# Layer 1 of a two-layer gated attention kernel: the two nearest prototypes taken from the products, their distances on ScalarE, residual rows in and results out two tiles at a time

## The reference, cut to what matters

```
def _L1_ffn_ref(x, prototypes, B, A, bias, temp):
    x2 = jnp.sum(xf * xf, axis=1, keepdims=True)
    p2 = jnp.sum(prototypes * prototypes, axis=1)
    d2 = x2 + p2[None, :] - 2.0 * (xf @ prototypes.T)
    dists = jnp.sqrt(jnp.maximum(d2, 0.0))
    t = jnp.maximum(jnp.abs(temp), 0.1)
    w = jax.nn.softmax(-dists / t, axis=1)
    topw, topi = jax.lax.top_k(w, 2)
    topw = topw / jnp.sum(topw, axis=1, keepdims=True)
    for tslot in range(2):
        idx = topi[:, tslot]
        h = jnp.einsum('nri,ni->nr', B[idx], xf)
        y = jnp.einsum('nor,nr->no', A[idx], h) + bias[idx]
        out = out + topw[:, tslot:tslot + 1] * y
...
x = x + jnp.tanh(g_xattn[1]) * _L1_xattn_ref(_layernorm(x, axis=-1), ctx_1024, ctx_1024, ...)
x = x + jnp.tanh(g_ffn[1]) * _L1_ffn_ref(_layernorm(x, axis=-1), ...)
```

## Time and profile before

| | us |
|---|---|
| median of 3 runs | 3044.14 |
| lowest and highest | 3039.18, 3046.79 |
| the profiled execution | 3044.48 |
| its span | 3042.8 |

### The profile page before, as it was taken

How to read it: one execution, slowest core, us unless ns; L and a number is a source line. 1 busy time by engine, 2 the same in 40 slices (tenths; PEclk the granted TensorE clock), 3 DMA queues, 4 the chain that set the end, 5 groups by cost and what they waited for, 6 DMA issues and landing times.

```text
span 3042.8 us, 96434 instructions
## 1 busy us (share of the span) xinstructions
PE 2739.6 (90%) x31534; PEld 2166.8 (71%) x31534; DVE 2507.4 (82%) x6126; ACT 1983.7 (65%) x4683; POOL 2089.8 (69%) x2777
## 2 busy tenths in 40 slices
PE   4888896899999999689699999999989999999996
PEld 2444444677777777557578888888878888888885
DVE  6877776688888888675689999899989989999885
ACT  2666666687777877575466666666656666666663
POOL 3893000567666676544388888888888888888886
PEclk9999998899999999899899999999999999999998
DMA  5987566223233232631567766666776767766663
GB/s 152 364 337 294 235 254 256 76 81 93 77 90 84 80 93 76 220 117 41 121 142 158 158 147 149 140 145 150 145 137 149 141 144 149 147 150 145 145 132 78
DMA packets 638943, 455.55 MB, mean 150 GB/s; under 512 B 389760, under 2 KB 612592, under 8 KB 633648
## 3 DMA queue, kind: packets, MB, share of 16 engines
q1 hardware_dynamic: 618288, 402.31, 52.2%
q0 software_dynamic: 7328, 23.40, 2.5%
q10 hardware_dynamic: 12960, 25.23, 2.2%
HBM read 235.08 MB, written 148.83 MB: 126 GB/s over the span
## 4 chain that ended last, share of the span: by engine, by line
PE 32%; DVE 6%; issue 4%; POOL 3%; SPq 2%; ACT 2%; DMA 1%; DVEq 0%; POOLq 0%; ACTq 0%
PE banks L150 10%; PE banks L152 9%; PE banks L151 9%; PE banks L1416 2%; DVE a_near L1540 2%; PE banks L1401 2%; SPq L1058 1%; DVE a_probT_lo L1492 1%; ACT a_qT_hi L1234 1%; DVE a_pick L1627 1%; DVE a_rsum L1504 1%; DVE a_wtop L1567 1%; POOL a_pn L1154 1%; DMA a_xnT<-a_xn_parts 0%; DMA a_hwT<-a_hw_parts 0%
## 5 line engine op out<-in xcount | busy, mean ns | idle before, releaser
L1234 ACT ACTIVATE a_qT_hi<-banks 128x512 f16<-128x512 f32 x252 | 150.4, 597 | 540.8 <-PE banks L152 540.8
L383 POOL TENSOR_TENSOR a_probT_lo<-a_expT,a_probT_hi 128x512 f16<-128x512 f32 x256 | 291.4, 1159 | 218.5 <-ACT a_probT_hi L466 218.5
L459 ACT ACTIVATE a_expT<-banks,a_top,w_score_scale 128x512 f32<-128x512 f32 (+1 forms) x384 | 272.4, 709 | 152.5 <-PE banks L550 146.1
L1154 POOL TENSOR_TENSOR a_pn<-a_prob,a_rsum 128x1024 f32<-128x1024 f32 (+1 forms) x256 | 310.2, 1233 | 5.8 <-DVE a_rsum L1506 5.8
L150 PE MATMUL banks<-a_xnT,w_q_hi 128*128 128x256 f16 x1024 | 281.2, 275 | 15.0 <-DMA a_xnT<-a_xn_parts 13.2
L150 PE MATMUL banks<-a_vo_front,a_probT_hi 128*128 128x256 f16 x1024 | 279.8, 273 | 9.4 <-DVE a_probT_lo L1492 6.5
L152 PE MATMUL banks<-a_xnT,w_q_lo 128*128 128x256 f16 x1024 | 280.6, 274 | 0.0
L151 PE MATMUL banks<-a_xnT,w_q_hi 128*128 128x256 f16 x1024 | 280.6, 274 | 0.0
L152 PE MATMUL banks<-a_vo_front,a_probT_lo 128*128 128x256 f16 x1024 | 279.7, 273 | 0.0
L151 PE MATMUL banks<-a_vo_front,a_probT_hi 128*128 128x256 f16 x1024 | 279.6, 273 | 0.0
L1490 DVE TENSOR_TENSOR a_qT_lo<-banks,a_qT_hi 128x512 f16<-128x512 f32 x252 | 172.0, 683 | 77.9 <-ACT a_qT_hi L1234 77.7
(11 more groups left out here) (380 smaller groups left out, 10177.7 us busy)
## 6 DMA issues: line engine op xcount, KB each, us to landing
vo<-kv_vo_out SPq DMA_DIRECT2D x38, 2048.0 KB, 8.1
a_vo_front<-vo SPq DMA_DIRECT2D x128, 512.0 KB
kt<-kv_k_out ACTq DMA_DIRECT2D x9, 2560.0 KB, 14.9
a_k<-kt SPq DMA_DIRECT2D x64, 308.0 KB, 3.5
kv_raw_e<-in_L_ffn_w POOLq DMA_DIRECT2D x16, 1024.0 KB, 8.9
a_x<-in_x SPq DMA_DIRECT2D x64, 256.0 KB, 2.9
a_y<-in_x SPq DMA_DIRECT2D x64, 256.0 KB, 2.7
x<-a_y SPq DMA_DIRECT2D x64, 256.0 KB, 2.8
```

What stands on the lines that cost most here:

```text
L383: pool.tensor_tensor(probT[b][1][:, first:end, :], expT[b][:, first:end, :], probT[b][0][:, first:end, :], ALU.subtract).then_inc(prob_rea ...
L459: act.activation(expT[1 - h][0:rows, first:end, :], bank, ACT.Exp, bias=top[0:rows, 0:1], scale=weights["score_scale"][0:rows, 0:1]).then_ ...
L1154: last = pool.tensor_tensor(keys_of(pn[h]), e[:, :, first:end], rsum[h][:, :].unsqueeze(2).broadcast_to([P, H, end - first]), ALU.mult)
L1234: act.activation(out, bank[:, 0:cols].rearrange("p (c s) -> p c s", c=out.shape[1]), ACT.Copy, scale=scale)\
```

## The change

`near` is gone. `nearest_two` looks for the largest of `dots` itself, and the row's squared length comes in later, on ScalarE, for the two found values alone: `square_gaps` computes relu(ysq - top) on 128x2 numbers. It stands in ScalarE's list in group 0 of every half, ahead of `norm2_log`, and waits for VectorE's `top_found` of tile t-6, which VectorE produces at the end of the half before. GpSimd's `top_weights` waits for it (`gap_ready`) and adds TINY where it had multiplied by -1. `ysq` holds four tiles instead of two. On VectorE a one-number memset takes the wait. The residual rows of both tiles of a batch are loaded by one DMA in h = 0, and both tiles are stored by one DMA in h = 1. The buffer for them holds 16 tiles in 8 pairs instead of 8 tiles.

```diff
-    SLOTS = 8
+    SLOTS = 16
+    PAIRS = SLOTS // TPB
...
+    LENGTHS = 4
...
-        def load_rows(t, slot, before):
-
-            need(sp, out_done[slot], before * 16)
-            sp.dma_start(y_sb[slot][:, :], src_rows[tile_at(t)]).then_inc(y_in[slot], 16)
+        def load_rows(i, slot, before):
+
+            pair = slot // TPB
+            need(sp, out_done[pair], before * 16)
+            sp.dma_start(y_pair[pair][:, :, :], src[batch_at(i)]).then_inc(y_in[pair], 16)
...
-                if live(i * TPB + h - 2, NT):
-                    load_rows(i * TPB + h - 2, *place(2, u, h, j))
+                if h == 0 and live(i - 1, NB):
+                    load_rows(i - 1, *place(2, u, 0, j))
...
-                if live(t, NT):
-                    slot = (TPB * u + h - LAG) % SLOTS
-                    need(sp, out_ready, t + 1)
-                    sp.dma_start(dst[tile_at(t)], y_sb[slot][:, :]).then_inc(out_done[slot], 16)
+                if h == 1 and live(i - LAG // TPB, NB):
+                    pair = (u - LAG // TPB) % PAIRS
+                    need(sp, out_ready, (i - LAG // TPB + 1) * TPB)
+                    sp.dma_start(dst[batch_at(i - LAG // TPB)], y_pair[pair][:, :, :]).then_inc(out_done[pair], 16)
...
             step = Steps(pool, top_step, t, TOP_STEPS)
-            need(pool, top_used, t)
-            pool.tensor_tensor(dist[:, :], top[:, 0:2], numbers[:, 2:3].broadcast_to([P, 2]), ALU.mult).then_inc(top_used, 1)
+            need(pool, gap_ready, t + 1)
+            kept = pool.tensor_tensor(dist[:, :], square[:, :], numbers[:, 2:3].broadcast_to([P, 2]), ALU.add)
             pool.tensor_copy(topf[:, :], topi[:, 0:2]).then_inc(top_ready, 1)
-            need(pool, top_used, t + 1)
+            step(kept)
...
+        def square_gaps(t, h, u):
+
+            n = (TPB * u + h - 6) % LENGTHS
+            need(act, top_found, t + 1)
+            need(act, ysq_done, t + 1)
+            need(act, more_ready, t)
+            act.activation(square[:, :], top[:, 0:2], ACT.Relu, bias=ysq[:, n:n + 1], scale=-1.0).then_inc(gap_ready, 1)
...
             need(act, ln2_inverse, t + 1)
-            need(act, near_ready, t - 1)
-            act.activation(ysq[:, h:h + 1], inv2[:, :], ACT.Identity, scale=mv2[:, 1:2]).then_inc(ysq_done, 1)
+            act.activation(ysq[:, n:n + 1], inv2[:, :], ACT.Identity, scale=mv2[:, 1:2]).then_inc(ysq_done, 1)
...
                     if g == 0:
                         prep(0)
+                        if live(t - 6, NT):
+                            square_gaps(t - 6, h, u)
                         if live(t - 4, NT):
                             norm2_log(t - 4)
...
-        def nearest_two(t, h):
-
+        def nearest_two(t):
+
+            need(dve, gap_ready, t)
             need(dve, dots_read, t + 1)
-            need(dve, ysq_done, t + 1)
-            nc.vector.tensor_scalar(near[:, :], dots[:, :], ysq[:, 1 - h:2 - h], -TINY, ALU.subtract, ALU.min)\
-                .then_inc(near_ready, 1)
-            need(dve, top_used, t)
-            hold(near_ready, t + 1)
-            nc.vector.max(top[:, :], near[:, :]).then_inc(top_found, 1)
+            nc.vector.memset(idle_top[:, :], 0.0)
+            nc.vector.max(top[:, :], dots[:, :]).then_inc(top_found, 1)
```

More of the change, by code:

```diff
@@ L773, in attention_ffn_phase @@
     vo_in = [sem(f"vo_in{p}") for p in range(2)]
-    out_done = [sem(f"out_done{s}") for s in range(SLOTS)]
-    y_in = [sem(f"y_in{s}") for s in range(SLOTS)]
+    out_done = [sem(f"out_done{s}") for s in range(PAIRS)]
+    y_in = [sem(f"y_in{s}") for s in range(PAIRS)]
     work_full = [sem(f"work_full{s}") for s in range(WORK)]
@@ L792, in attention_ffn_phase @@
         sem("yn_ready"))
-    ln_log, ln_root, more_ready, first_weight = sem("ln_log"), sem("ln_root"), sem("more_ready"), sem("first_weight")
+    gap_ready, ln_log, ln_root, more_ready, first_weight = sem("gap_ready"), sem("ln_log"), sem("ln_root"), sem("more_ready"), sem("first_weight")
     ln2_inverse = sem("ln2_inverse")
     yn_hi, yn_lo, dots_read = sem("yn_hi"), sem("yn_lo"), sem("dots_read")
[L796 to L799, removed]
+    top_found, topi_found, top_ready = sem("top_found"), sem("topi_found"), sem("top_ready")
+    top_step, wtops_ready, picked, wsel_ready = (
+        sem("top_step"), sem("wtops_ready"), sem("picked"), sem("wsel_ready"))
     low_ready, hw_ready, hw_hi, hw_lo, wselT_hi, wselT_ready, out_ready = (
@@ L875, in gpsimd_numbers @@
         def gpsimd_numbers(self):
-            for n, number in enumerate((-0.5, 0.5, -1.0, 1.0)):
+            for n, number in enumerate((-0.5, 0.5, TINY, 1.0)):
                 pool.memset(numbers[:, n:n + 1], number).then_inc(numbers_set, 1)
@@ L945, in attention_ffn_phase @@
     quarter = [sb(f"quarter{p}", [P, H, FRONT // 4]) for p in range(2)]
-    y_sb = [sb(f"y{s}", [P, D]) for s in range(SLOTS)]
+    y_pair = [sb(f"y{s}", [P, TPB, D]) for s in range(PAIRS)]
+    y_sb = [y_pair[s // TPB][:, s % TPB, :] for s in range(SLOTS)]
     minus_mean2, shift2 = sb("minus_mean2", [P, 1]), sb("shift2", [P, 1])
@@ L952, in attention_ffn_phase @@
     ynT = [sb(f"ynT{p}", [P, 2 * DC, P], F16) for p in range(2)]
-    ysq = sb("ysq", [P, TPB])
-    dots, near = sb("dots", [P, NPROTO]), sb("near", [P, NPROTO])
+    ysq = sb("ysq", [P, LENGTHS])
+    dots, idle_top = sb("dots", [P, NPROTO]), sb("idle_top", [P, 1])
     top, topi, topf = sb("top", [P, 8]), sb("topi", [P, 8], U32), sb("topf", [P, 2])
-    dist, dgap, late, wtop = sb("dist", [P, 2]), sb("dgap", [P, 1]), sb("late", [P, 1]), sb("wtop", [P, 2])
+    dist, square, dgap, late, wtop = sb("dist", [P, 2]), sb("square", [P, 2]), sb("dgap", [P, 1]), sb("late", [P, 1]), sb("wtop", [P, 2])
     more, euler, decay = sb("more", [P, 1]), sb("euler", [P, 1]), sb("decay", [P, 1])
@@ L1127, in _ @@
         bodies(sp, body)
-        for s in range(SLOTS):
-            sp.wait_ge(out_done[s], 16 * (NT // SLOTS))
+        for s in range(PAIRS):
+            sp.wait_ge(out_done[s], 16 * (NB // PAIRS))
     @block.gpsimd
@@ L1528, in prototype_products @@
             bank = full(i, ("low", h, 0))
-            need(dve, near_ready, t)
+            need(dve, topi_found, t)
             need(dve, low_ready, t * LU + 1)
@@ L1534, in prototype_products @@
                 .then_inc(dots_read, 1)
[L1536 removed]
+        def nearest_two(t):
+            need(dve, gap_ready, t)
             need(dve, dots_read, t + 1)
[L1539 to L1544 removed]
+            nc.vector.memset(idle_top[:, :], 0.0)
+            nc.vector.max(top[:, :], dots[:, :]).then_inc(top_found, 1)
         def nearest_index(t):
             hold(top_found, t + 1)
[L1549 removed]
+            nc.vector.max_index(topi[:, :], top[:, :], dots[:, :]).then_inc(topi_found, 1)
         def prepare(i, p, h, part):
@@ L1572, in add_residual @@
             slot, before = place(3, u, h, j)
-            need(dve, y_in[slot], (before + 1) * 16)
+            need(dve, y_in[slot // TPB], (before + 1) * 16)
             nc.vector.scalar_tensor_tensor(out=y_sb[slot][:, :], in0=bank[:, 0:D], scalar=out_scale,
@@ L1638, in body @@
                 if live(t - 5, NT):
-                    nearest_two(t - 5, h)
+                    nearest_two(t - 5)
                     nearest_index(t - 5)
@@ L2961, in flamingo_layers @@
             wq, score_scale, ffn = weights1.results()
-            layer1 = attention_ffn_phase(nc, layer, psum, const, batches(x1), tiles(x1), tiles(out), keys(DC, KV_COLS // P),
+            layer1 = attention_ffn_phase(nc, layer, psum, const, batches(x1), tiles(x1), batches(out), keys(DC, KV_COLS // P),
                                          (out_front, out_back), wq, score_scale, ffn,
```

8 lines of the change are left out of this document (4 added, 4 removed).

## The result

The changed kernel takes 3069.71 us (median of 4 runs, 3068.77 to 3074.18), the kernel before 3042.8 (4 runs beside it, 3039.18 to 3046.79): ratio 1.0086, 95% interval 1.0072 to 1.0099. The forecast was 3073; the stated range, 3008 to 3090 us, was wide enough to hold the faster rival too, so what follows asks whether the chain of waits behind the 3073 is the one that the trace shows. The profiled execution took 3069.01 us, its span is 3067.3, 24.5 us longer than before. Inside the span the starts of GpSimd's addition for the low half of xn (L1161 before, L1163 now) place these 24.5 us: 0.4 before the first of them that both traces show in steady work (1573.62 and 1574.05), 4.1 in the next 12 bodies, 11.3 in the 32 of the loop, 7.6 in the next 13, 1.2 behind the last one. Nothing is lost ahead of layer 1.

What follows compares the result with a forecast made beforehand. TensorE sets the pace, with VectorE deciding up to `attend`. Losses of 15.3, 9.0 and 3.8 us, together 28.1, with 0.8 for the last store 29 us, on 3044.48 give 3073 us; own range 3061 to 3090, stated range 3008 to 3090.

Steps and rivals of the forecast that it cites:

- faster rival: In h = 0 wsel stays ahead of L1161, near's gain is real, 0.55 us a loop body: 3016 us; chance 0.28.
- chain of waits: In h = 0 L1161 holds wsel, MAX8 follows, ScalarE waits for MAX8, attend comes 0.51 us later.
- Who sets the pace: From 2000 to 2400 us TensorE, busy 375.24 of 400 us; its waits for probT_lo, 15.2 us, are where the change acts.
- ScalarE's activation in h = 1 and L1171: GpSimd's L1171 waits for ScalarE's hw_parts in h = 1, so square_gaps makes it 0.18 us later relative to TensorE.
- GpSimd's idle time before L1161: GpSimd absorbs the 0.18 us shift there; its idle time shrinks from 0.61 to about 0.45 us.
- wsel loses by a margin of 0.02: wsel starts 0.59 us after L1146's end, L1161 0.61; a 0.18 us shift puts L1161 first, wsel held 1.16 us.
- L1264: On ScalarE in h = 0, behind the waiting square_gaps: starts at 2124.9 instead of 2123.43, 1.45 us later.
- `attend`: On TensorE in h = 0, behind VectorE's last probT_lo: 0.51 us later in the loop, 0.64 in the written-out bodies.
- ScalarE's slack of 0.94: ScalarE's probT_hi of group 2 has 0.94 us to spare in h = 0; only a delay beyond that delays attend.
- The sum: Loop 30 x 0.51 = 15.3, last bodies 14 x 0.64 = 9.0, first 6 x 0.64 = 3.8, last store 0.8: 29 us.
- The DMA: Transposed hw comes 0.5 to 1.2 us earlier, giving nothing; last store 0.8 us more. Rival, larger loads delay transposes: 3060 us, 0.02.

Runs made afterwards that it cites:

- farther_weight_first: The changed kernel with wtop moved one place up in VectorE's list, ahead of the aggregation of the second normalisation: 3035.63 us, 0.9966.
- norm_log_later: The changed kernel with norm_log(i + 2) moved behind weighed_high on ScalarE, directly ahead of norm_root: 3019.85 us, 0.9927.
- before_norm_log_later: The kernel before with only norm_log(i + 2) moved behind weighed_high on ScalarE: 3055.16 us, 1.0034.

## Why the prediction was right

- *Who sets the pace.* Right: what TensorE's matmuls lose is the wait for probT_lo, 12.1 us more from 2000 to 2400 us, less the 4.2 us of waits for transposes that it covers; the wait for the last query block stayed.
- *ScalarE's activation in h = 1 and L1171.* I said 0.18 us later. From L1163 (2132.20) to L1173 (2149.04) are 16.84 us, before 16.21. `attend` is 0.44 of the 0.63 later, 0.19 are left. The activation's pitch is 2133.91 - 2133.70 = 0.21.
- *GpSimd's idle time before L1161.* I said 0.61 to about 0.45; it is 0.43.
- *wsel loses by a margin of 0.02.* Right: it starts 0.16 after L1163, 0.59 after L1148's end as before, and takes 1.12. The Trainium skill (SBUF — State Buffer, "Who interferes with whom") says that issue order decides who blocks. The trace agrees, as far as its starts can tell the order: in farther_weight_first wtop is 0.15 us long when it is 0.02 ahead, 0.59 when 0.04 behind.
- *L1264.* I said 1.45 us later. It starts 1.71 us after L1163, before 0.30: 1.41.
- *`attend`.* I said 0.51 in the loop. It starts 4.72 us after L1163, before 4.28: 0.44. ScalarE's slack of 0.94 held: 1.38 us later probT_hi, 0.44 later `attend`. The memset, for which I had added 0.10, runs beside MAX8; that is most of the difference.
- *The sum.* First bodies 3.8 forecast, 4.1 measured. Loop 15.3 against 11.3: 30 bodies with 0.42 instead of 0.51, and 1.2 us won at the loop's turn, which I had set at nothing. Last bodies 9.0 against 7.6, 13 with 0.58 instead of 14 with 0.64. The end 0.8 against 1.2. Together 29 against 24.5 in the profiled executions (of these, 0.4 lie ahead of the first body counted); the medians differ by 26.9. The loop's term was 4 us too large and that of the last bodies 1.4, and neither touches the chain of waits.
- *The DMA.* I said it gives nothing and costs nothing: right within 3.5 us.
- *The faster rival* was real. If wsel stays ahead I gave 3016 us, 0.55 us of a loop body. norm_log_later has 3019.85, and the loop bodies that farther_weight_first wins take 23.03 us against 23.84 before (medians of 30), 0.81 less: more than I gave.
- *What I would have got wrong.* I priced the margin with GpSimd's idle time alone and took the 0.59 us from L1148's end to wsel as fixed. It is 0.59 or 0.28, according to whether L1148 holds wtop. In this change that didn't matter, since wtop was behind in both kernels; it sank the expectation for before_norm_log_later.
- The Trainium skill's rule that relu belongs on VectorE (ScalarE: Activation LUTs, "Rules for kernel authors") speaks against the move itself. The runs don't bear that out: with L1163 behind `weigh` in both, the kernel with the activation on ScalarE takes 3033.32 us and the one with near on VectorE 3036.83, and with the activation and norm_log later in ScalarE's list it comes down to 3008.9.

Not tried: the last store alone, the loop's turn, and an activation in only one of the two halves, which would show by itself that the one in h = 1 decides the race.

## What to carry to other kernels

When an instruction is taken off an engine, look for the next one that can inherit its stall, and ask who waits behind that one: here a hold on near stopped only VectorE, the same hold on wsel stopped ScalarE too. A step moved to another engine brings its wait along, so place it where its input is surely there, or move its producer ahead of what can be held. And where two engines meet within 0.1 us, compare the starts in several bodies of each kind before trusting a margin: loop and written-out bodies of one kernel can fall on different sides.

## What the hardware showed that I had not expected

- A multiplication of VectorE on one number a partition (wtop, 128x1) takes 0.12 to 0.15 us when it comes ahead of GpSimd's L1148 and 0.55 to 0.59 when it starts 0.04 to 0.07 us behind it: what counts is GpSimd's instruction, not its own size.
- GpSimd pays little when it comes second: L1163 is 1.16 us long when it holds wsel, 1.16 when, in farther_weight_first's loop, wsel starts 0.15 ahead of it, and at most 1.28 us (norm_log_later, before_norm_log_later) when the two start within 0.02 us of each other and wsel is the free one.
- MAX8 takes 0.18 to 0.20 us in every run, whatever GpSimd does meanwhile, so it can stand where ScalarE needs it: moving it ahead of wsel was worth 48 us against the changed kernel.
